# Two gated writes: the delta product in one fp32r pass over 96 stacked rows, and the inverse sums spread over 32 rows

## The reference

```python
def rat_write(res, y, wod_w, wab_w, wab_b, du_w, du_b):
    o_d = y @ wod_w.T
    A_B = y @ wab_w.T + wab_b
    out, delta_low = o_d[..., :H], o_d[..., H:]              # delta_low: 8 values of a token
    A_logit, B_proj, B_skip = ...                            # 48, 48 and 16 values
    delta = softplus(delta_low @ du_w.T + du_b)              # 8 (+1 for the bias) -> 512
    A_neg = -softplus(A_logit)
    A_bar = exp(delta * A_neg)
    B_bar = (A_bar - 1.0) / (A_neg - SSM_EPS) * B_proj
    return hs * [A_bar, 1] + out * [B_bar, delta * B_skip]
```

## Time and profile before

| | |
|---|---|
| median of 3 runs (lowest, highest) | 2239.14 us (2226.57, 2247.09) |
| the profiled execution | 2235.39 us, span 2233.3 us |
| busy: PE, DVE, POOL, ACT | 94%, 66%, 53%, 49% of the span |
| granted TensorE clock, mean | 0.971 of full speed |
| the first write | about 686 to 950 us from the start |
| the second write | about 1300 to 1645 us |

### The profile page before, as it was taken

One profiled execution on the slowest core, in us unless ns is written; L12 is line 12 of the kernel. 1 busy time (PEld: TensorE's weight loads), 2 busy tenths in 40 slices (PEclk: granted clock), 3 DMA queues, 4 the chain that ended last, 5 costly groups with the idle time before them and its releaser, 6 DMA issues.

```text
span 2233.3 us, 34661 instructions
## 1 busy us (share of the span) xinstructions
PE 2109.5 (94%) x11176; PEld 1732.0 (78%) x11176; DVE 1479.1 (66%) x1950; ACT 1087.5 (49%) x1700; POOL 1185.9 (53%) x717
## 2 busy tenths in 40 slices
PE   6998889999998999799999999999889999999999
PEld 4777766666666888778888899999678877888887
DVE  6778766777765788644665527766877665757663
ACT  3445447888884677732221235666533222223231
POOL 0111137999997677600000047777567676666464
PEclk9999998999998899899999999999999999999999
DMA  5677862343324666567898747887998699897796
GB/s 189 208 241 246 261 194 82 98 106 97 100 68 127 243 217 216 189 197 241 295 330 275 250 159 288 303 298 292 333 347 296 217 316 312 284 303 257 257 326 203
DMA packets 259629, 516.93 MB, mean 231 GB/s; under 512 B 20979, under 2 KB 136691, under 8 KB 240965
## 3 DMA queue, kind: packets, MB, share of 16 engines
q1 hardware_dynamic: 259524, 515.60, 69.2%
HBM read 359.81 MB, written 155.45 MB: 231 GB/s over the span
## 4 chain that ended last, share of the span: by engine, by line
PE 50%; DVE 5%; DMA 4%; issue 3%; ACT 3%; POOL 2%; SPq 0%; DVEq 0%; POOLq 0%; ACTq 0%
PE s_m_psG L2342 8%; PE s_m_psU L2342 8%; PE s_psF L2938 7%; PE s_psF L2939 7%; PE s_psF L2940 7%; PE s_w_psA L1906 4%; PE s_w_psB L1906 4%; DMA s_f_xs<-xnT 2%; PE s_w_psR L1405 1%; PE s_w_psT L1938 1%; POOL s_f_xs L2894 1%; DMA s_f_xl<-xnT 1%; DVE s_w_ab L1674 1%; PE s_w_psT L1923 1%; DVE s_f_acc L2835 1%
## 5 line engine op out<-in xcount | busy, mean ns | idle before, releaser
L1052 POOL TENSOR_TENSOR s_a_pl<-s_a_pf,s_a_ph 128x1024 fp32r<-128x1024 f32 x128 | 301.8, 2391 | 22.2 <-ACT s_a_pf L1009 22.1
L2894 POOL TENSOR_TENSOR s_f_xs<-s_f_xl,s_f_xs 128x1024 f32<-128x1024 f32 x80 | 204.1, 2552 | 144.6 <-DMA s_f_xs<-xnT 144.4
L2078 POOL TENSOR_TENSOR s_w_yl<-s_w_y,s_w_yh 128x1024 fp32r<-128x1024 f32 x32 | 76.0, 2397 | 365.7 <-ACT s_w_yh L1986 365.7
L947 DVE TENSOR_REDUCE s_a_mx<-s_psS 128x1 f32<-128x512 f32 (+2 forms) x248 | 179.3, 754 | 98.1 <-PE s_psS L875 97.7
L2767 ACT ACTIVATE s_f_xh<-s_f_xs 128x1024 fp32r<-128x1024 f32 x80 | 84.9, 1061 | 287.5 <-POOL s_f_xs L2894 287.5
L2818 DVE TENSOR_TENSOR s_f_xl<-s_f_xs,s_f_xh 128x1024 fp32r<-128x1024 f32 x80 | 109.4, 1368 | 156.4 <-ACT s_f_xh L2767 156.4
L2938 PE MATMUL s_psF<-s_f_wh,s_f_xh 128*128 128x512 f32 x448 | 175.5, 392 | 9.0 <-DVE s_f_acc L2835 7.7
L448 POOL TENSOR_TENSOR s_q_qk<-s_q_ra,s_q_rb 128x1024 f32<-128x1024 f32 x16 | 37.7, 2358 | 272.7 <-DVE s_q_rb L691 272.7
L1006 ACT ACTIVATE s_a_ph<-s_psX 128x1024 fp32r<-128x1024 f32 (+1 forms) x160 | 150.6, 941 | 52.6 <-PE s_psX L903 48.8
L2939 PE MATMUL s_psF<-s_f_wl,s_f_xh 128*128 128x512 f32 x448 | 175.1, 391 | 0.0
L2940 PE MATMUL s_psF<-s_f_wh,s_f_xl 128*128 128x512 f32 x448 | 175.0, 391 | 0.0
(11 more groups left out here) (335 smaller groups left out, 6388.7 us busy)
## 6 DMA issues: line engine op xcount, KB each, us to landing
s_f_xl<-xnT SPq DMA_DIRECT2D x112, 512.0 KB, 5.5
s_f_xs<-xnT SPq DMA_DIRECT2D x80, 512.0 KB, 7.0
s_q_xt<-xT SPq DMA_DIRECT2D x16, 1024.0 KB, 7.5
s_q_xc<-xP SPq DMA_DIRECT2D x16, 1024.0 KB, 9.9
hsD<-s_q_hs SPq DMA_DIRECT2D x16, 1024.0 KB, 4.8
s_w_hin<-hsD SPq DMA_DIRECT2D x16, 1024.0 KB, 5.1
hs<-s_w_res SPq DMA_DIRECT2D x16, 1024.0 KB, 3.8
s_m_raw<-giT SPq DMA_DIRECT2D x32, 512.0 KB, 5.7
```

What stands on the lines that cost most here:

```text
L947: dve.tensor_reduce(mx[:, slot % 2, qi:qi + 1], psS[:, off:off + (qi + 1) * P], AX, ALU.max).then_inc(mx_ok, 1)
L1052: pool.tensor_tensor(pl[:, r, cols], pf[:, j - 1], ph[:, r, cols], ALU.subtract).then_inc(pl_ok, 1)
L2894: pool.tensor_tensor(xs[i % 3][:], xl[u % 4][:].bitcast(F32), xs[i % 3][:], ALU.add if product(u)[1][1][2] > 0 else ALU.subtract).then_inc ...
```

## The change

In both writes the delta product is made with fp32r operands in one product over 96 rows: three groups of 32 rows, of which 9 are used and the others are zero. The stationary operand `dlT` holds the high, the low and again the high part of the 9 delta values; the moving operand `du` holds the high part of the weights twice and their low part. For that, DVE splits the 9 columns of `pa` into a zeroed tile `zd` (`split_low`: a copy of 128 x 2 x 9 and, after it, a subtraction of 128 x 9), and TensorE transposes `zd` (96 columns) in place of 9 columns of `pa`. In the first write the spread of the inverse sums gets the same treatment: `rr` is loaded twice, over 32 rows, DVE makes `rs` from it (`split_inverse`: high part in 16 rows, low part in 16), and `pick` becomes an fp32r tile of 32 rows. In a turn of the first write `spread_sums` now stands before `turn_small` on TensorE. Some semaphores of the first write are released for the second.

```diff
+LOW = 32
-        du = sb("w_du", [S0, H])
+        du = sb("w_du", [3 * LOW, H], F32R)
-        pick = sb("w_pick", [NH, KH, P])
+        pick = sb("w_pick", [2 * NH, KH, P], F32R)
-        rr = sb("w_rr", [NH, B, L])
+        rr = sb("w_rr", [2 * NH, B, L])
+        rs = sb("w_rs", [2 * NH, B, L], F32R)
-        dlT = sb("w_dlT", [S0, P])
+        dlT = sb("w_dlT", [3 * LOW, P], F32R)
+        zd = sb("w_zd", [P, 3 * LOW])
...
         def prepare_sync(sp, i):
-                sp.dma_start(du[:], io["du1"]).then_inc(small_in, 16)
+                sp.wait_ge(du_zero, 1)
+                for j in range(3):
+                    sp.dma_start(duraw[j * LOW:j * LOW + S0], io["du1"]).then_inc(du_in, 16)
...
         def prepare_scalar(act):
-            act.activation(pick[:].rearrange("h g (n d) -> h (g n) d", d=HD),
-                           spread(k["ident"][0:NH, 0:NH].unsqueeze(2), NH, NH, HD), ACT.Copy).then_inc(ready, 1)
         def prepare_gpsimd(pool):
+            pool.memset(duraw[:], 0.0).then_inc(du_zero, 1)
...
         def load_inverse(sp, b):
-            sp.dma_start(rr[:, b], io["oR"][b * NH:(b + 1) * NH]).then_inc(rr_in, 16)
+            for j in range(2):
+                sp.dma_start(rr[j * NH:(j + 1) * NH, b], io["oR"][b * NH:(b + 1) * NH]).then_inc(rr_in, 16)
+        def split_inverse(dve, b):
+            dve.wait_ge(rr_in, 32 * (b + 1))
+            dve.tensor_copy(rs[:, b], rr[:, b]).then_inc(rs_ok, 1)
+            dve.wait_ge(rs_ok, 2 * b + 1)
+            dve.scalar_tensor_tensor(rs[:, b], rr[:, b], second[0:2 * NH, :], rs[:, b], ALU.mult, ALU.subtract).then_inc(rs_ok, 1)
+        def prepare_tables(dve):      # pick, second and du, five instructions
...
         def vector_ahead(dve, i):
+            if i == 0:
+                prepare_tables(dve)
             if i == 1:
                 invert_sums(dve, 0)
+            if i == 3:
+                split_inverse(dve, 0)
...
         def tensor(pe, after):      # first write
-                inv = rr[:].rearrange("h b t -> h (b t)")[:, ds(s.at(P), P)]
+                inv = rs[:].rearrange("h b t -> h (b t)")[:, ds(s.at(P), P)]
             def turn_small(s, q, live):
-                pe.wait_ge(pa_ok, count(s - 1, 2, 1))
+                pe.wait_ge(z_ok, count(s - 1, 2, 2))
-                pe.transpose(psL, pa[:, q, 0:S0], k["ident"][:]).then_inc(dl_mm, 1)
+                pe.transpose(psL, zd[:], k["ident"][:]).then_inc(dl_mm, 1)
-            pe.wait_ge(rr_in, 16)
+            pe.wait_ge(rs_ok, 2)
             def body(s, p, live):
+                if live(0):
+                    spread_sums(s)
                 if live(1):
                     turn_small(s, q, live)
-                if live(0):
-                    spread_sums(s)
...
         def vector(dve):      # first write
+            def split_low(s, q):
+                dve.wait_ge(pa_ok, count(s - 1, 2, 1))
+                if (s - 2).exists():
+                    dve.wait_ge(dl_mm, count(s - 2, 1, 1))
+                cells = zd[:].rearrange("p (g j) -> p g j", j=LOW)
+                dve.tensor_copy(cells[:, 0:3:2, 0:S0].bitcast(F32R), spread(pa[:, q, 0:S0].unsqueeze(1), P, 2, S0)).then_inc(z_ok, 1)
+                dve.wait_ge(z_ok, count(s - 1, 2, 1))
+                dve.tensor_tensor(cells[:, 1, 0:S0].bitcast(F32R), pa[:, q, 0:S0], cells[:, 0, 0:S0], ALU.subtract).then_inc(z_ok, 1)
             def body(s, p, live):
                 if live(4):
                     statistics(s)
+                if s.reg is None and s.off == 5:
+                    split_inverse(dve, 1)
                 if live(2):
                     update(s, p, 0)
+                if live(1):
+                    split_low(s, q)
                 if live(4):
                     normalise(s)
...
         def vector(dve, after, amid):      # second write: the same split_low, first in the turn
             def body(s, p, live):
+                if live(2) and live(1):
+                    split_low(s, p)
                 if live(3):
                     update(s, 1 - p)
```

More of the change, by code:

```diff
@@ L1098, in build_write1 @@
         bet = sb("w_bet", [P, 2 * KH])
+        second = sb("w_second", [P, 1])
+        duraw = nc.alloc_sbuf_tensor_at("s3_w_duraw", [3 * LOW, H], F32, offset=zone["keep"] + 2 * KH * NW * 4 + NW * 4 + P * 4)
         sb = shelf(nc, "s3_", zone["tables"], zone["XB"])
@@ L1140, in build_write1 @@
         w_hi, prep, w_lo, ready = sem("w_hi"), sem("prep"), sem("w_lo"), sem("ready")
+        du_zero, du_in, du_ok, pick_ok, rs_ok, z_zero, z_ok = (sem(n) for n in
+            ("du_zero", "du_in", "du_ok", "pick_ok", "rs_ok", "z_zero", "z_ok"))
         def prepare_sync(sp, i):
@@ L1622, in vector @@
             att["outputs_out"](dve)
+            dve.memset(zd[:], 0.0).then_inc(z_zero, 1)
+            dve.wait_ge(z_zero, 1)
+            dve.wait_ge(ready, 7)
+            def split_low(s, q):
[6 more added lines that the diff above has]
+                dve.tensor_tensor(cells[:, 1, 0:S0].bitcast(F32R), pa[:, q, 0:S0], cells[:, 0, 0:S0], ALU.subtract).then_inc(z_ok, 1)
             def statistics(s):
@@ L1816, in sync_ahead @@
                 sp.dma_start(braw[:], io["bsm2"]).then_inc(small_in, 16)
-                sp.dma_start(du[:], io["du2"]).then_inc(small_in, 16)
+                sp.wait_ge(du_zero, 1)
+                for j in range(3):
+                    sp.dma_start(duraw[j * LOW:j * LOW + S0], io["du2"]).then_inc(du_in, 16)
             if i >= RW:
@@ L1840, in vector_ahead @@
                     dve.wait_ge(out, 16 * mlp["spare"])
+                dve.wait_ge(cleared, 1)
+                dve.memset(duraw[:], 0.0).then_inc(du_zero, 1)
             if i == RW:
@@ L1911, in turn_small @@
             def turn_small(s):
-                pe.wait_ge(pa_ok, count(s - 2, 2, 1))
-                pe.wait_ge(one_ok, 3)
+                pe.wait_ge(z_ok, count(s - 2, 2, 2))
                 if (s - 5).exists():
                     pe.wait_ge(t_ev, count(s - 5, 4, 3))
-                pe.transpose(psT[0][0:S0, 0:P], pa[:, s.off % 2, 0:S0], k["ident"][:]).then_inc(dl_mm, 1)
+                pe.transpose(psT[0][0:3 * LOW, 0:P], zd[:], k["ident"][:]).then_inc(dl_mm, 1)
             def deltas(s):
@@ L2123, in vector, with split_low @@
             dve.memset(pa[:, :, 0:1], 1.0).then_inc(one_ok, 1)
+            dve.memset(zd[:], 0.0).then_inc(z_zero, 1)
+            dve.wait_ge(z_zero, 1)
+            dve.wait_ge(one_ok, 3)
+            def split_low(s, p):
+                dve.wait_ge(pa_ok, count(s - 2, 2, 1))
+                if (s - 3).exists():
+                    dve.wait_ge(dl_mm, count(s - 3, 1, 1))
+                cells = zd[:].rearrange("p (g j) -> p g j", j=LOW)
+                dve.tensor_copy(cells[:, 0:3:2, 0:S0].bitcast(F32R), spread(pa[:, p, 0:S0].unsqueeze(1), P, 2, S0)).then_inc(z_ok, 1)
+                dve.wait_ge(z_ok, count(s - 2, 2, 1))
+                dve.tensor_tensor(cells[:, 1, 0:S0].bitcast(F32R), pa[:, p, 0:S0], cells[:, 0, 0:S0], ALU.subtract).then_inc(z_ok, 1)
             def update(s, q):
@@ L2180, in body @@
                     statistics(s, 1 - p)
-            steps(dve, TILES, LAST, 2, body, LAST + 1, after=after)
+            last = Step(None, TILES + 1, TILES)
+            steps(dve, TILES, LAST, 2, body, LAST + 1, after=lambda i: after(i, lambda: split_low(last, 1)))
         first = Step(None, 0, TILES)
@@ L2840, in vector_ahead @@
                 lo_x(dve, 1)
-                for n in range(HK):
+                lo_piece(dve, 0)
+                lo_piece(dve, 1)
+                split()
+                for n in range(2, HK):
                     lo_piece(dve, n)
@@ L2967, in build_rest @@
     spent = TAKEN[held:]
+    first = len(TAKEN)
     w1 = build_write1(nc, io, k, zone, qkv, att)
+    spent += [handle for handle in TAKEN[first:] if not any(handle is kept for kept in w1["kept"])]
     plane = build_plane(nc, io, k, zone)
```

54 lines of the change are left out of this document (39 added, 15 removed).

## The result

| | before | with the change |
|---|---|---|
| median (lowest to highest), 4 runs each | 2237.49 us (2226.57 to 2247.09) | 2282.78 us (2277.39 to 2289.60) |
| profiled execution, span | 2233.3 us | 2281.8 us |
| ratio | | 1.0224, 95% interval 1.0187 to 1.0261 |

A forecast was written before the change was run, and what follows sets the result against it. Both writes were taken as PE's on average, warm first-write turns as bound by DVE and ACT. Terms 2.4 - 1.8 + 3.0 - 2.1 - 0.7 - 8.8 - 9.1 + 0.5 gave -16.6 us: 2222 us, range 2206 to 2243.

The forecast's parts named there:

- the price and the cover of `split_low`: Both writes: two short DVE instructions cost about 0.4 us; in the second write DVE's 4.50 us wait covers them, so 0.
- The last sign of the prediction: Second write: a POOL or DVE wait in front of PE's products would show the forecast wrong in another way.
- Preparation: First write's tables between attention copies, with a 4.11 us wait following, plus small loads and a memset: +0.5 us.
- Start of the first write: `split_inverse(0)` behind the last attention copy moves the first L1757 from 687.44 to 689.85: +2.4 us.
- Delta product: Both writes: one 96-row fp32r product moves the chain on by 0.23 us instead of 1.05, saving 0.82 a turn.
- the third rival: Second write: the POOL and DVE loop takes the gain, the 9.1 becomes 4 or less: 2228 us; chance 0.12.
- 9.1: Second write: thirteen turns set by PE each save 0.7 us, -9.1 us in all.
- Warm turns of the first write: About ten full-clock turns, each longer by DVE's 0.4 us less 0.1 slack: +3.0 us in all.
- Filling and cold turns: First write: PE's savings in three filling turns, -1.8 us, three cold half-clock turns, -2.1, and the drain, -0.7.
- The clock: First write: a shorter gap before the read leaves one clock fall for three, 2 x 4.4 us saved: -8.8.
- The slower rival: First write, between last psB product and read: less PE work brings 8 more clock falls, about 2262 us; chance 0.08.
- dear pair: The pair on DVE costs 1 us instead of 0.4, or its waits hold up update 1: +6, 2228 us; chance 0.04.

The follow-up runs named there:

- e9: The changed kernel with the subtraction of the second write's split_low left out, only its copy kept: 2259.57 us.
- e5: Separate test computing nothing of the layer: nine forms of DVE instruction run alone and beside POOL; SBUF-to-SBUF copy 2.45 against 0.43 us, forms with PSUM 0.69 each time.
- e3: Both writes changed, but in the second ACT copies the columns and DVE makes the low part after the transpose from PSUM: 2251.14 us, ratio 1.0099 to before.
- e4: The changed kernel with the first table instruction (L1235) made by POOL before the attention instead of DVE: 2289.65 us in one run.
- e7: Kernel before with only the first write changed, tables made by POOL and ACT (reduction on DVE), split_low behind the normalisation: 2244.68 us, ratio 1.0062.
- e6: Kernel before with only the second write changed, its low part made after the small transpose as in e3: 2227.13 us, ratio 0.9985.
- e11: e7 with the first write's split_low call taken out, so its delta values are left out of the product: 2233.43 us, ratio 1.0001 to before.
- e2: Kernel before with the change in the second write alone: 2265.76 us, ratio 1.0152.
- e8: Both writes changed with all three repairs: tables off DVE, first split_low behind the normalisation, second write's low part after the small transpose: 2238.45 us, ratio 1.003 to before.
- e10: The changed kernel with the subtraction of the second write's split_low done twice, one behind the other: 2300.32 us.

## Why the prediction was wrong, step by step

- **The step that failed** is the price and the cover of `split_low`: "Two of them cost about 0.4 us", and in the second write "The new pair on DVE stands first in its turn, inside the 4.50 us that DVE waits for POOL there: 0". Measured: up to 5.1 us for the pair (L2200 and L2202 at 1543.72) and +26.4 us in the stage. The cover was real for the copy alone, which ends with the POOL instruction that DVE waits for there (0.3 us a turn, e9). The subtraction behind it meets the next one, L2144, is held for nearly all of it, and TensorE's small transpose waits up to 2.95 us for that: some 2.1 us a turn, and the falls of the clock on top. The price came from L1636, an aggregation, which is among the forms that aren't held (e5). e3, e5 and e9 show that the hold is the cause. The last sign of the prediction, a DVE wait in front of TensorE's work in the second write, is the one that came.
- **Preparation, "+0.5"**: 10.01 us for one instruction (e4 shows that the first one behind it that can be held takes it over). The same error; the wait of 4.11 us that was to cover it came too late and is shorter.
- **Start of the first write, +2.4** for `split_inverse`: between the end of the last copy and L1757 lie 3.3 us here (698.66 to 701.99) and 3.1 in e7, 0.45 before. Mechanism right, 0.3 to 0.5 too small: the four spreading products took 1.08 us at a granted clock of 0.50 (0.45 was taken), behind a wait of 2.77 us.
- **Delta product, 0.82 saved a turn**: right, 1.05 to 0.25. With the hold away the turn of the second write falls by 0.56, not 0.7: the loop of POOL and DVE takes the rest, as the third rival had it in part. Over the stage only 2.9 us came of it (e6), not 9.1.
- **Warm turns of the first write, +0.3**: +0.55 to +1.2, and 0.8 where nothing is held (e7 against e11). There the pair lasts 0.5 us, near the 0.4 taken, but costs more than it lasts. TensorE's saving was worth 0.05 us a turn, as good as nothing, as said.
- **Filling and cold turns, -1.8, -2.1 and -0.7**: no run separates them from the falls of the clock; the first write lasts 213.9, 200.2 and 203.9 us in the three profiles of its old code. The prediction's "In a cold turn PE is never idle" is not quite what its row says, 17.44 of 17.80 us.
- **The clock, -8.8**: not seen in the change. The windows of the changed kernel show the fall to half clock three times from 766 on (near 768, 814 and 890), like before:

```profile
814.00:826.00 12.00, 11.52 (x56) 10.79 (x57) 10.74 (x17) 7.36 (x17) 8.93 (x8) 0.57 0.72 262
```

  Nor can a count of it be put down to an edit. Profiles of e2 and e6, whose first write is that of before, show one and two such falls where before shows three. With the holds away the first write of e7, e8 and e11 shows one, one and no fall between 764 and 903, the two of 3.41 us and not 10.24; that is the way the prediction meant, but one profile each doesn't show it. The slower rival (more falls) didn't come at its place; falls came in the second write instead, behind the wait for the subtraction, and took some 7 us. The first cause of the loss is a mechanism that none of my rivals named; the "dear pair" had 1 us and a chance of 0.04, and a time above 2261.5 had 0.08.

Could the trace before have told? Yes. The feed-forward has a DVE subtraction of two SBUF tiles; its group in the kernel before (minimum, median and maximum in ns), and DVE and POOL where it is longest in their timelines:

```profile
L2818 DVE TENSOR_TENSOR s_f_xl<-s_f_xl,s_f_xh x32: 1212/1250/4419, 1578.2 to 2082.3; 128x1024 fp32r<-128x1024 f32 x32
```

```profile
1578.21 6.19 DVE L2818 TENSOR_TENSOR s_f_xl<-s_f_xl,s_f_xh 128x1024 fp32r<-128x1024 f32 x2
...
1592.47 1.23 DVE L2818 TENSOR_TENSOR s_f_xl<-s_f_xl,s_f_xh 128x1024 fp32r<-128x1024 f32 x1 [0.26 <-ACT s_f_xh L2767]
```

```profile
1579.06 4.26 POOL L2109 TENSOR_TENSOR s_w_t<-s_w_hin,s_w_g 128x1536 f32<-128x1536 f32 x1
```

The same instruction takes 1.23 us where POOL is idle as it starts, and two of them 6.19 where POOL works; POOL's L2109, 3.50 elsewhere, takes 4.26 beside them. A factor of 3.6 between minimum and maximum of one group was the thing to ask about.

The Trainium skill has the rule, in "SBUF — State Buffer", section "Who interferes with whom": DVE's second pair of SBUF ports is GpSimd's only one, and a copy in a two-port mode, or an operation with two SBUF inputs against a GpSimd instruction that reads SBUF, needs it for its whole length, so that the one that comes second is blocked; a reduction never does. e4 (reduction 0.15 us, cast 9.60) and e5 agree with it, form by form, and so does the order of starts in e5. The prediction weighed two other pages of the skill and not this one. The page speaks of waiting until the other's instruction is finished; L1235 waited for five, which its words don't foretell.

## What to carry to other kernels

Before giving DVE a short instruction, look at where its operands lie and at what POOL does at that moment: a copy from SBUF to SBUF, or an operation on two SBUF tiles, is held for the rest of POOL's instruction, however few its elements. "DVE waits for POOL here" covers one such instruction at best (0.3 us a turn in e9), and the one behind it meets POOL's next (2.1 us). When a stage's turns have two lengths, look at the granted clock of each before looking for a second cause. The way out is an operand in PSUM (here the split done behind the transpose, 0.28 us) or ACT for the copy, and a price read from an instruction of the same form, by its maximum beside its median.

## What the runs showed of the hardware

- The hold depends on the form: SBUF to SBUF copy 2.45 against 0.43 us, two SBUF operands 2.19 against 0.17; with a PSUM operand an instruction is not held, nor are the reciprocal, the aggregation and the reduction (e4, e5).
- It is shown as a long busy time of the held instruction, so that DVE looked busier by 34 us in the same 259 us.
- It can outlast one instruction: 10.01 and 9.60 us behind five of POOL's that follow each other without a gap. In the second write the copy ended between two of POOL's that the profile shows without a gap (L2175 ends at 1526.43, L2144 starts at 1526.39). What tells these apart stays open.
- Which of two comes first decides: in e5, started 20 to 30 ns ahead of POOL, the same forms weren't held, and POOL lost 0.3 to 0.5 us instead beside those of 512 columns.
- In the second write of the change, TensorE's waits of 2.93 to 2.95 us were followed by 3.41 us at a granted clock of 0.50 in four cases of five, those of 2.34 to 2.36 in none; e3 and e9, without such waits, have no fall in those turns. In e2, e4 and e10 other waits have a fall behind them too, so the length of the wait alone doesn't decide.
- An fp32r product on 96 rows and 512 columns moves TensorE's stream on by 0.25 us, like one on 128 rows (0.23).
